# Two-layer gated cross-attention and mixture-of-experts kernel: key and query groups 1 to 3 loaded within the attention stage, second layer's key projection in two PSUM banks

## The reference, cut to what matters

```python
x = x + tanh(g_xattn[0]) * xattn0(layernorm(x), ctx)   # q, k, v, softmax(q k^T / 4) v, output projection
x = x + tanh(g_ffn[0])   * ffn0(layernorm(x))          # shared SwiGLU expert + the top-1 of 8 experts
x = x + tanh(g_xattn[1]) * xattn1(layernorm(x), ctx)   # as xattn0, with a two-matrix ReLU MLP at its end
x = x + tanh(g_ffn[1])   * ffn1(layernorm(x))          # top-2 of 8 experts, then a layernorm of mixed + x
```

## Time and profile before

| | us |
|---|---|
| median of 3 runs (lowest, highest) | 1779.24 (1774.21, 1781.85) |
| the profiled execution: its time | 1781.89 |
| its span | 1779.6 |
| ACT busy | 927.7 (52%) |
| PE busy | 1405.0 (79%) |
| DVE busy | 558.5 (31%) |

### The profile page before, as it was taken

How to read it: one execution, slowest core, us unless ns; L and a number is a source line. 1 busy time by engine, 2 the same in 40 slices (tenths; PEclk the granted TensorE clock), 3 DMA queues, 4 the chain that set the end, 5 groups by cost and what they waited for, 6 DMA issues and landing times. The chain is left out here.

```text
span 1779.6 us, 29932 instructions
## 1 busy us (share of the span) xinstructions
PE 1405.0 (79%) x12336; PEld 657.0 (37%) x12336; DVE 558.5 (31%) x1301; ACT 927.7 (52%) x1110; POOL 148.1 (8%) x144
## 2 busy tenths in 40 slices
PE   6469999999949986998247999999999440899920
PEld 4223333333327543555122334333343240566610
DVE  7401242324234022221352123223232340232347
ACT  3269999999922111111136987969879000222200
POOL 3100000000001500000410000000000006000042
PEclk9779999999977976999678999999999755999965
DMA  5750011000017101111826000000000072111122
GB/s 157 176 158 24 19 26 25 24 17 26 26 43 289 48 29 45 42 42 38 164 76 192 22 20 23 17 22 18 25 22 18 12 269 97 45 54 60 54 85 71
DMA packets 95370, 116.51 MB, mean 65 GB/s; under 512 B 11714, under 2 KB 80934, under 8 KB 94464
## 3 DMA queue, kind: packets, MB, share of 16 engines
q1 hardware_dynamic: 90192, 98.13, 18.6%
q0 software_dynamic: 4608, 12.59, 2.4%
q10 hardware_dynamic: 432, 3.83, 1.1%
HBM read 73.32 MB, written 36.70 MB: 62 GB/s over the span
## 5 line engine op out<-in xcount | busy, mean ns | idle before, releaser
L921 ACT ACTIVATE arena<-ps 128x1024 f32<-128x1024 f32 x832 | 767.5, 1127 | 92.5 <-PE ps L842 92.5
L842 PE MATMUL ps<-arena 99*32 99x512 bf16 x6656 | 440.3, 382 | 37.6 <-PEq L724 36.4
L857 PE MATMUL ps<-arena 128*32 128x512 f32 x3328 | 442.9, 605 | 1.5 <-ACT arena L921 1.5
L842 PEld LDWEIGHTS ps<-arena 99*32 99x32 bf16 x6656 | 187.1, 97 | 378.0 <-issue 283.9
L1427 PE MATMUL ps<-arena,work 128*128 x340 | 166.6, 625 | 22.6 <-DVE work L1488 22.4
L933 DVE COPY work<-ps 128x512 f32<-128x512 f32 x32 | 22.1, 691 | 489.8 <-PE ps L857 489.8
L857 PEld LDWEIGHTS ps<-arena 128*32 128x32 f32 x3328 | 70.1, 108 | 158.3 <-ACT arena L921 147.8
L1445 PE MATMUL ps<-arena,work 128*128 x496 | 117.4, 379 | 1.5 <-ACT work L1475 1.5
L1471 ACT ACTIVATE work<-work 128x512 f32<-128x512 f32 x39 | 24.6, 630 | 167.1 <-DVE work L1499 167.1
L1445 PEld LDWEIGHTS ps<-arena,work 128*128 128x128 f32 x496 | 94.1, 190 | 40.3 <-issue 30.7
L937 DVE RECIPROCAL work<-work 128x512 f32<-128x512 f32 x32 | 107.3, 3352 | 1.1
(11 more groups left out here) (158 smaller groups left out, 1070.8 us busy)
## 6 DMA issues: line engine op xcount, KB each, us to landing
arena<-in_ew SPq DMA_DIRECT2D x16, 512.0 KB, 7.6
work<-list_x SPq DMA_DIRECT2D x62, 128.0 KB, 2.1
list_y<-work SPq DMA_DIRECT2D x62, 128.0 KB, 1.7
arena<-q_img SPq DMA_DIRECT2D x40, 192.0 KB
q_img<-work SPq DMA_DIRECT2D x24, 256.0 KB, 2.6
arena<-q_img SPq DMA_DIRECT2D x40, 128.0 KB
list_x<-zero SPq DMA_DIRECT2D x1, 5120.0 KB, 17.5
k_img<-work SPq DMA_DIRECT2D x24, 208.0 KB, 2.3
```

Source lines behind the costliest of these rows:

```text
L842: last = nc.tensor.matmul(ps[i * VW:(i + 1) * VW, buf + j, :], k2[0:ROWS + SHIFT, h, at:at + VW], q2[0:ROWS + SHIFT, h, :], start=True, st ...
L857: last = nc.tensor.matmul(ps[j * VW:(j + 1) * VW, 6 + g % 2, :], v_aug[:, c, HG * g + j, :], probs[:, w % 2, j, :], start=(c == 0), stop=( ...
L921: nc.scalar.activation(probs[:, w % 2, 2 * half:2 * half + 2, :], ps[:, buf:buf + 2, :], ACT.Exp).then_inc(s_exp, 1)
```

## The change

In both layers the loads of key and query groups 1 to 3 are issued by SP at the start of the attention block, ahead of the weights and the zeros. Gone are SP's query loads and ACT's key loads at the end of the preparation, and, in the block that brings the rows back, the second layer's key groups 1 to 3; group 0 is still loaded there, and SP waits in that block for the stores of the keys, for which it waited at the end of the routing block before. The last block of rows loads no queries. The unsafe branch loads the keys for itself. In the second layer's key projection the two halves of a block use banks 7 and 5, the squares have two buffers (the second in `w1`), and PE sums the squares of a block after it has projected the next one.

```diff
--- before.py
+++ after.py
@@ -203,7 +203,8 @@
         full1[0], at = view(work, at, [KD, KB])
         full1[1], _ = view(work, 0, [KD, KB])
         rest1, _ = view(work, KD * QB, [KD, KB])
-        squares1, _ = view(arena, (E + 1) * (2 * KD * F + 4 * D), [KD, KB], BF16)
+        squares1 = [view(arena, (E + 1) * (2 * KD * F + 4 * D), [KD, KB], BF16)[0],
+                    view(w1[:, :, :].rearrange("p k n -> p (k n)"), 0, [KD, KB], BF16)[0]]
 
         TS = 2 * NT
         lg = sb("lg", [P, NT, E])
@@ -482,8 +483,6 @@
                     load_q2(sp, 0, 0)
                     store(Q0 + 2)
                     store(Q0 + 3)
-                    for g in range(1, NG):
-                        load_q2(sp, 0, g)
                     sp.wait_ge(s_w, 16 * (5 if L.mlp else 3))
 
                 @block.scalar
@@ -545,10 +544,6 @@
                         values(range(7, NC))
                         act.wait_ge(s_gate, 32)
                         nc.scalar.activation(tgate[:, :], gates[:, :], ACT.Tanh)
-                        for i in range(2):
-                            act.wait_ge(s_po[i], 96)
-                        for g in range(1, NG):
-                            load_k2(act, 0, g, s_k2[g])
 
                 @block.tensor
                 def _(pe):
@@ -711,15 +706,15 @@
                 sem(f"head_q{l}"), sem(f"max_scores{l}"), sem(f"max_taken{l}"), sem(f"max_turned{l}"),
                 sem(f"max_copied{l}"), sem(f"max_split{l}"), sem(f"shift_stored{l}"))
             s_m1, s_m2, s_m3 = [sem(f"max_part{l}_{i}") for i in range(3)]
-            s_re = sem(f"q2_again{l}")
+            s_re, s_ku = sem(f"q2_again{l}"), sem(f"k2_for_max{l}")
             q_head = q2.rearrange("p h s -> p (h s)")[:, 0:S]
             def keys_in(eng, groups):
 
                 for g in groups:
-                    if l == 0:
+                    if l == 1 and g == 0:
+                        eng.wait_ge(s_kin[1], 64)
+                    else:
                         eng.wait_ge(s_k2[g], 48 if g else 64)
-                    elif g == 0:
-                        eng.wait_ge(s_kin[1], 16 * (3 * NG + 1))
 
             with nc.Block() as block:
                 def asked(eng):
@@ -730,8 +725,9 @@
                     with asked(sp):
                         for i in range(2):
                             sp.wait_ge(s_po[i], 24 * Q0 + 96)
-                        for g in range(NG):
-                            sp.wait_ge(s_q2[g], 16 * 4)
+                        for g in range(1, NG):
+                            load_k2(sp, l, g, s_ku)
+                        sp.wait_ge(s_q2[0], 16 * 4)
 
                         def load_head(h):
                             for i, _, qj, n in RUNS:
@@ -752,14 +748,14 @@
                             load_head(h)
                             store_head(h)
                         sp.wait_ge(s_md, 16 * SHIFT * H)
-                        for g in range(NG):
-                            load_q2(sp, 0, g, s_re)
-                        sp.wait_ge(s_re, 16 * 4 * NG)
+                        load_q2(sp, 0, 0, s_re)
+                        sp.wait_ge(s_re, 16 * 4)
 
                 @block.tensor
                 def _(pe):
                     with asked(pe):
-                        keys_in(pe, range(NG))
+                        keys_in(pe, [0])
+                        pe.wait_ge(s_ku, 48 * (NG - 1))
 
                         def head(h, first):
                             pe.wait_ge(s_hq, 48 if first else h * 48 + 48)
@@ -1006,14 +1002,19 @@
                     def body(b, first):
                         if not first:
                             gather_heads(b - 1, NG - 1)
-                        at = (b + 1) % NB * QB
                         for g in range(NG):
 
-                            sp.wait_ge(s_qk, b * STEPS + 2 * NC * (g + 1))
-                            load_q2(sp, at, g)
+                            if b < NB - 1:
+                                sp.wait_ge(s_qk, b * STEPS + 2 * NC * (g + 1))
+                                load_q2(sp, (b + 1) * QB, g)
                             if g < NG - 1:
                                 gather_heads(b, g)
 
+                    for i in range(2):
+                        sp.wait_ge(s_po[i], 24 * Q0 + 96)
+                    for g in range(1, NG):
+                        load_q2(sp, 0, g)
+                        load_k2(sp, l, g, s_k2[g])
                     if l == 0:
                         load_wk(sp, 1)
                         load_wv(sp, 1)
@@ -1021,8 +1022,6 @@
                     n = L.tiles + 1
                     sp.dma_start(list_x[l].rearrange("(t p) d -> p t d", p=P),
                                  zero[:, :].unsqueeze(1).broadcast_to([P, n, D])).then_inc(s_fill, 16)
-                    for i in range(2):
-                        sp.wait_ge(s_po[i], 24 * Q0 + 96)
                     for b in range(NB):
                         body(b, b == 0)
                     gather_heads(NB - 1, NG - 1)
@@ -1032,7 +1031,7 @@
                         sp.wait_ge(s_wv[1], 48)
                         sp.wait_ge(s_wq[1], 48)
                     for g in range(NG):
-                        sp.wait_ge(s_q2[g], (NB + 1) * 16 * 4)
+                        sp.wait_ge(s_q2[g], NB * 16 * 4)
 
         def moe(L):
             l = L.n
@@ -1085,8 +1084,6 @@
                         for n in range(4):
                             sp.wait_ge(s_kl, n + 1)
                             store_parts(sp, k_img[1], part1[n % 2], slice(n * KB, (n + 1) * KB), False, s_kd[n % 2])
-                        for i in range(2):
-                            sp.wait_ge(s_kd[i], 96)
                     for q in s_e:
                         sp.wait_ge(q, 16 * (3 if l == 0 else 4))
 
@@ -1108,13 +1105,13 @@
                     def k_item(n):
 
                         for ko in range(KD):
-                            if n or ko:
-                                pe.wait_ge(s_kh, n * KD + ko)
-                            project_k(1, ko, n, 7).then_inc(s_kp, 1)
+                            if n:
+                                pe.wait_ge(s_kh, (n - 1) * KD + ko + 1)
+                            project_k(1, ko, n, (7, 5)[ko]).then_inc(s_kp, 1)
 
                     def k_norm(n):
                         pe.wait_ge(s_ks, KD * (n + 1))
-                        norm_sums(ps[:, 3, n * 4 * H:(n + 1) * 4 * H], squares1, KC).then_inc(s_kn, 1)
+                        norm_sums(ps[:, 3, n * 4 * H:(n + 1) * 4 * H], squares1[n % 2], KC).then_inc(s_kn, 1)
 
                     for b in range(NB):
                         if b >= 2:
@@ -1172,8 +1169,8 @@
                         pe.wait_ge(s_sy, NT)
                         k_item(0)
                         for n in range(1, 4):
+                            k_item(n)
                             k_norm(n - 1)
-                            k_item(n)
                         k_norm(3)
 
                 @block.scalar
@@ -1191,11 +1188,12 @@
                             if n >= 2 and ko == 0:
                                 act.wait_ge(s_kl, n - 1)
                                 act.wait_ge(s_kd[n % 2], 48)
-                            nc.scalar.activation(full1[n % 2][:, ko, :], ps[:, 7, 0:KB], ACT.Copy).then_inc(s_kf, 1)
-                            if n and ko == 0:
-                                act.wait_ge(s_kn, n)
-                            nc.scalar.activation(squares1[:, ko, :], ps[:, 7, 0:KB], ACT.Square).then_inc(s_ks, 1)
-                            nc.scalar.activation(part1[n % 2][0][:, ko, :], ps[:, 7, 0:KB], ACT.Copy).then_inc(s_kh, 1)
+                            src = ps[:, (7, 5)[ko], 0:KB]
+                            nc.scalar.activation(full1[n % 2][:, ko, :], src, ACT.Copy).then_inc(s_kf, 1)
+                            if n >= 2 and ko == 0:
+                                act.wait_ge(s_kn, n - 1)
+                            nc.scalar.activation(squares1[n % 2][:, ko, :], src, ACT.Square).then_inc(s_ks, 1)
+                            nc.scalar.activation(part1[n % 2][0][:, ko, :], src, ACT.Copy).then_inc(s_kh, 1)
 
                     def shared_act(b, f):
 
@@ -1575,8 +1573,9 @@
                 def _(sp):
                     if l == 0:
                         spread_ones(sp, s_kin[1], 2)
-                        for g in range(NG):
-                            load_k2(sp, 1, g, s_kin[1])
+                        for i in range(2):
+                            sp.wait_ge(s_kd[i], 96)
+                        load_k2(sp, 1, 0, s_kin[1])
                     else:
                         dst = out.rearrange("o (t p) d -> p (o t) d", p=P)
                         for b in range(NB):
```

## The result

| | before | after |
|---|---|---|
| median, beside each other on one chip | 1776.72 (4 runs, 1766.27 to 1781.85) | 1734.31 (4 runs, 1728.37 to 1739.57) |
| the profiled execution: its time | 1781.89 | 1739.17 |
| its span | 1779.6 | 1736.7 |

The account below looks back on a forecast made before the run. The 832 exponentials (767.5 of 1779.6 us) bound the kernel; gains lie between stages. A + B + C + D = 26.0 + 17.5 + 14.1 + 4.2 = 61.8 off 1781.89 gives 1720.1, less 2.65 for the median: 1717.4 us, range 1704 to 1737.

Parts of the forecast that it names:

- A: First preparation to attention: with the loads moved out, PE's first score at 78.2 us, gain 26.0 us.
- I take 2.3, because the 8.3 lie under a DMA backlog: First passage into the attention: priced at the second layer's 2.3 us, not the first layer's 8.3.
- Rival 1: First passage into the attention takes 8.3 us for its own reasons: gain 20.0 there, 1723.4 us; chance 0.15.
- rivals 2 and 3: Attention stage: loading starves PE of instructions (1753.4 us, chance 0.06); keys come late (1788 us, chance 0.03).
- B: Second layer's key projection: PE projects while ACT copies, next block's first load at 669.2 instead of 686.71, gain 17.5 us.
- I take full clock: Key projection: PE keeps full clock throughout; half clock from 652 on would cost 4.4 us more, gain 13.1.
- rival 4: Key projection: PE runs at half clock; 1721.8 us, chance 0.12.
- C: Bringing the rows back: nine of 12 key loads go, end at 890.5 instead of 904.6, gain 14.1 us (6.8 to 20.4).
- it begins by 859.8 even if: Bringing back: latest start of DVE's first add, if ones, key group and four gathers pass first in 10.9 us; 858 taken.
- D: Second preparation: 12 issues on SP go, first score at 944.7 instead of 948.89, gain 4.2 us (3 to 5).

Follow-up runs that it names:

- a_backlog: Changed kernel with ACT also issuing the nine loads of key groups 1 to 3 at the end of the second preparation; 1757.77 us (1 run).
- c_order: Changed kernel with SP issuing key group 0 ahead of the row of ones in the bringing-back block; 1718.66 us (1 run).
- b_one_bank: Changed kernel with the second layer's key projection back to one bank and one buffer of squares; 1746.2 us (1 run).
- best_landed: Changed kernel with the edits of c_both and b_three_sets, and SP waiting for the query stores after the first preparation; 1699.66 us (6 runs).
- c_both: Changed kernel with the row of ones and key group 0 moved to the start of the second preparation; 1710.17 us (4 runs).
- b_three_sets: Changed kernel with a third buffer set for the parts of the second layer's keys; 1729.94 us (4 runs).
- a_undone: Changed kernel with the first layer's loads of groups 1 to 3 back at the end of its preparation; 1757.73 us (1 run).

## Why the prediction was right or wrong

The range held the time and the direction was right; of the 18.9 us that the forecast's gain was too large, 11.1 are in the terms of the sum and 7.8 in stretches that the change doesn't touch.

**A, 22.5 instead of 26.0.** The step that failed is "I take 2.3, because the 8.3 lie under a DMA backlog". The backlog is real: under it the same passage took 8.3 and 13.3 us. But without it 5.6 are left (4.6 to 5.7 in the nine experiments that keep this part as it is, 5.2 and 3.2 in the two with the extra wait), because this passage has a fetch of instructions in it and the second layer's has none. The two prices differed in two things at once, and I gave the whole difference of 6.0 to one: TensorE's branch takes 6.27 us before, 3.62 now and 0.35 in the second layer, so the backlog's part was 2.7 and the fetch's own 3.3. Rival 1 ("8.3 for its own reasons") gave 20.0 and was a little nearer to the truth than the forecast. The loads in the attention cost nothing, as forecast: the exponentials keep 0.92 us at a DMA share of 1.01, no wait of the scores on a DMA shows, and rivals 2 and 3 did not come. SP was held 13.3 us by the next block's queries behind the zeros (15.0 in the second layer), and nobody waited for it.

**B, 16.8 instead of 17.5.** That this came out so near is partly luck: two steps missed and nearly cancel. The first is "I take full clock". DVE ended 22.6 us after PE's start instead of 20.4, since the clock stayed at half after ACT's wait: rival 4 for two of the four halves that it priced. The next load came 1.7 us after DVE's end (645.82 - 644.12) instead of 3.2. The wait for the `k_img` stores was foreseen, and its end was placed at 11.4 us after PE's start where it was 10.65. That it also takes the clock, and so costs 5.2 us, was allowed for only as rival 4 and in the low end of B.

**C, 6.8 instead of 14.1, exactly the low end.** The step that failed is "it begins by 859.8 even if" the row of ones, the key group and four gathers have to pass first, "10.9 us" at 174 GB/s; I called 858 near the late end. The first add came at 21.0 us instead of 14.7. The bound counted 1.9 MB, and 2.85 passed between 808 and 823; the 0.95 more are an estimated 5.0 us at that stretch's 190 GB/s, and the add came 4.6 us after the bound. It left out that POOL goes on issuing gathers, so that eleven and not three shared the engines with what the add waited for; no run held POOL back to test this by itself. It also charged the row of ones by its bytes: measured alone it costs 7.1 us of the first add, where 0.15 MB at 174 GB/s are 0.9. The rest, 34.8 us from the first add to the next block, was nearly right (32.5 to DVE's end forecast, 33.4 measured). That the gain is the low end to the tenth is chance: 1.0 won at the first add and 0.9 lost behind it.

**D, 4.6 instead of 4.2**, from a passage of 2.2 us and a preparation shorter by some tenths.

**The rest.** From the first score to the key projection the changed kernel took 539.8 us, and the twelve experiments 528.9 to 542.9; from the second layer's first score to the end it took 840.5, and the experiments 827.7 to 844.7 (without a_backlog, whose edit reaches into it). The attentions hardly vary: the first takes 423.5 to 426.6 us in all kernels, the second 474.0 to 475.3 but for c_order, b_one_bank and a_backlog (477.2, 477.3 and 478.3). What varies most is the first routing block up to the key projection, 104.3 to 118.0 us, and it goes with the clock granted there: 0.93 in c_order and best_landed (104.3 and 104.4 us), 0.87 in c_both (110.6), 0.86 in the changed kernel (115.4), 0.85 before and in a_backlog (118.0); only b_three_sets (109.3 at a clock of 0.92) lies off that order. The second routing block up to the tile loop's first load (87.2 to 91.9) and the last block, whose issues of the output take 40.7 to 51.9, vary too. The profiled execution of the changed kernel was among the slower ones there (91.6 and 48.65; 87.3 and 43.75 before). Why code that no edit touches gets another clock, and what varies in the last block, is open. It means that times of two kernels which are some 10 us apart say little here, and the stretches say more.

## What to carry to other kernels

A bound on a wait for a transfer should count everything that will be issued until it lands, the later transfers of the same queue too, and a copy within few partitions by its measured landing and not by its bytes; the cheapest cure is to move such loads to a stretch that waits for no DMA, which gained 13 us here (14.0 in the block, 0.9 given back in the next). A wait in front of TensorE costs its own length and then the clock: 3.1 us of wait cost 4.1 to 5.2. Before the price of a block change is carried from one place to another, look whether the instruction queues have packets in one and not in the other.

## What the hardware showed that I had not expected

- TensorE's branch over code that had to be fetched took 3.62 us with the DMA engines free, 6.27 and 11.21 us under a backlog of loads (before, a_undone), and 0.35 us where nothing had to be fetched.
- Copies of 48.8 KB within one partition took 6.8 us to land, and three at once, keeping some twelve engines busy, moved no more than one DMA on three (0.03 and 0.04 MB in 2 us). Beside the one DMA a gather's packet took 0.44 us instead of 0.16; beside the three it took 0.12, but 25 packets passed instead of 64.
- A copy of 0.15 MB within three partitions took 5.3 to 8.1 us from first packet to last wherever it stood in the program.
- Nine key loads on ACT's queue stretched six stores on SP's queue from 6.26 to 15.98 us, though the queues differ.
